# A four-layer kernel on one core: an early one-column GELU, another order on GpSimd, and a copy moved to VectorE

## The reference, cut to what matters

```
f1: windowed attention: q, k, v = x @ w; tau = sigmoid(q.k / sqrt(8)) over the 16 tokens before;
    msg = tau.v; y = x + msg @ wo; layernorm
f2: softmax attention over the batch groups, out projection, layernorm; then 8 experts:
    top 2 of the router's softmax, the larger index wins; gelu(h @ w1[e] + b1[e]) @ w2[e] + b2[e]
    of that expert; layernorm(h + moe)
f3: state-space layer: layernorm, in-projection, causal convolution of 4, silu,
    dt = softplus(..), scan over 256 tokens with 16 states, * silu(z), out projection, residual
f4: h = silu(x @ w1) * (x @ w2); h = gelu(h @ h1); h = gelu(h @ h2); h @ w3   (hidden size 512)
```

## Time and profile before

| what | us |
|---|---|
| median of 3 runs | 908.96 |
| the three runs | 908.96, 910.29, 899.03 |
| profiled execution, its own time | 912.69 |
| its span in the trace | 910.9 |
| PE busy | 782.0 (86%) |
| DVE busy | 655.5 (72%) |
| ACT busy | 586.7 (64%) |
| POOL busy | 441.0 (48%) |
| mean granted clock of TensorE | 0.917 |

### The profile page before, as it was taken

How to read it: one execution, slowest core, us unless ns; L and a number is a source line. 1 busy time by engine, 2 the same in 40 slices (tenths; PEclk the granted TensorE clock), 3 DMA queues, 4 the chain that set the end, 5 groups by cost and what they waited for, 6 DMA issues and landing times.

```text
span 910.9 us, 21586 instructions
## 1 busy us (share of the span) xinstructions
PE 782.0 (86%) x8256; PEld 661.9 (73%) x8256; DVE 655.5 (72%) x1974; ACT 586.7 (64%) x1118; POOL 441.0 (48%) x776
## 2 busy tenths in 40 slices
PE   4978863899999999878768679999999999989996
PEld 4877752789989898867546457777778777767885
DVE  3587763777999999763699958686776867775532
ACT  4586861356767676746787569595867949555641
POOL 2477664233656565455588735436353533434101
PEclk9997985559999999999786889999999999999998
DMA  8400001200000000000000000000000000000000
GB/s 271 146 26 20 21 19 51 56 1 2 3 2 3 2 3 2 2 2 1 1 1 0 1 1 1 1 1 13 1 13 1 2 11 1 13 0 12 13 1 24
DMA packets 22406, 16.95 MB, mean 19 GB/s; under 512 B 2848, under 2 KB 20640, under 8 KB 22048
## 3 DMA queue, kind: packets, MB, share of 16 engines
q1 hardware_dynamic: 21296, 14.95, 5.4%
q10 hardware_dynamic: 1008, 0.63, 0.3%
HBM read 11.38 MB, written 4.19 MB: 17 GB/s over the span
## 4 chain that ended last, share of the span: by engine, by line
PE 56%; DVE 20%; ACT 9%; POOL 8%; issue 6%; DMA 1%; ACTq 0%; POOLq 0%; SPq 0%; DVEq 0%
PE ps L1716 9%; PE ps L1718 8%; PE ps L1717 8%; PE ps L1729 7%; PE ps L1796 6%; PE ps L2161 3%; DVE wall L1375 3%; PE ps L1735 2%; PE ps L1711 2%; PE ps L2020 2%; ACT tau L706 1%; ACT hbd L688 1%; PE ps L1789 1%; PE ps L2074 1%; PE ps L1820 1%
## 5 line engine op out<-in xcount | busy, mean ns | idle before, releaser
L1716 PE MATMUL ps<-h_h,wh_h 128*128 128x512 f32 x256 | 106.2, 415 | 1.4 <-DVE raw L1514 1.2
L1718 PE MATMUL ps<-h_l,wh_h 128*128 128x512 f32 x256 | 101.0, 395 | 0.0
L1717 PE MATMUL ps<-h_h,wh_l 128*128 128x512 f32 x256 | 100.8, 394 | 0.0
L1796 PE MATMUL ps<-w_e,he 128*128 128x128 f32 x512 | 78.2, 286 | 12.7 <-ACT he L738 12.3
L1796 PEld LDWEIGHTS ps<-w_e,he 128*128 128x128 f32 x512 | 67.0, 196 | 17.4 <-ACT he L738 16.9
L1729 PEld LDWEIGHTS ps<-mov,hbd 32*128 32x128 f32 x2048 | 77.7, 230 | 1.3 <-issue 1.3
L1729 PE MATMUL ps<-mov,hbd 32*128 32x32 f32 (+1 forms) x2048 | 76.8, 306 | 1.0 <-issue 1.0
L584 POOL TENSOR_TENSOR term<-term 128x224 f32<-128x224 f32 (+2 forms) x48 | 37.9, 790 | 79.0 <-DVE term L1406 76.5
L738 ACT ACTIVATE he<-ps,pp 128x256 f32<-128x256 f32 x128 | 58.6, 472 | 21.2 <-PE ps L1718 19.7
L1514 DVE SCALAR_TENSOR_TENSOR raw<-ps,pp,gate 128x512 f32<-128x512 f32 x32 | 23.8, 749 | 49.5 <-ACT gate L921 49.3
L1375 DVE TENSOR_TENSOR wall<-dec,wall 128x224 f32<-128x224 f32 (+6 forms) x112 | 48.7, 435 | 14.6 <-ACT dec L876 11.3
(11 more groups left out here) (299 smaller groups left out, 2522.8 us busy)
## 6 DMA issues: line engine op xcount, KB each, us to landing
x<-in_x SPq DMA_DIRECT2D x16, 128.0 KB
w_h<-in_w_h SPq DMA_DIRECT2D x2, 1024.0 KB, 8.0
x<-x SPq DMA_DIRECT2D x16, 128.0 KB, 1.8
xB<-x SPq DMA_DIRECT2D x32, 64.0 KB
out_x<-xB SPq DMA_DIRECT2D x32, 64.0 KB
w_m<-in_w_m SPq DMA_DIRECT2D x3, 256.0 KB, 3.5
stage_negsel<-in_c_negsel SPq DMA_DIRECT2D x1, 512.0 KB, 4.9
xB<-in_w_e SPq DMA_DIRECT2D x1, 512.0 KB, 6.0
```

The lines of the kernel that those rows point to most:

```text
L1716: pe.matmul(dst, a_h, b_h, start=start, stop=True, skip_group_check=True)
L1717: pe.matmul(dst, a_l, b_h, start=False, stop=True, skip_group_check=True)
L1718: return pe.matmul(dst, a_h, b_l, start=False, stop=True, skip_group_check=True)
L1796: last = pe.matmul(ps[:, ACC, P * c:P * c + P], he[e % 2][:, P * c:P * c + P], w_e2[:, e, :], start=False, stop=True, skip_group_check=True)
```

## The change

Three edits that do not touch each other:

1. A new tile `gelu_one` of one column. In each expert step ScalarE takes the GELU of the first column of the constant tile `half` into it, between `le` and the third expert's `gelu(n, l, 2)`, whose waits come after it. Nothing reads the result.
2. GpSimd in the last stage. Where a block enters and n < 16, `input_scale` comes first in the step, ahead of `rstd_and_shift` (before: after it). In odd steps from 5 on, `scales(n + 4)` comes after `skips(n)` and `stored(n - 2)` (before: ahead of both). Step 16 and the even steps' `scales` stay as they were.
3. The query's copy from PSUM to `mov` in the first stage leaves ScalarE and is done by VectorE at the end of `values`, behind the transpose to `vT`, with a wait for `a_qk_ps`; it still counts up `a_qT`.

```diff
--- before.py
+++ after.py
@@ -259,6 +259,7 @@
         hT = chan("hT")
 
 
+        gelu_one = sb("gelu_one", [P, 1])
         negsel = sb("negsel", [P, NE, P], F32R)
         b_e2 = sb("b_e2", [P, D])
         w_router = sb("w_router", [P, NE])
@@ -613,23 +614,26 @@
                 entering, leaving = block_of(n, 4), block_of(n, 7)
                 if n == 0:
                     products(1)
+                if entering is not None and n < NB:
+                    input_scale(entering)
                 if have(-2):
                     c_ln2.rstd_and_shift(pool, chain, eps, half, minus, (n - 2) % 4, n - 1)
                 if n == NB:
-                    input_scale(block_of(n, 4))
+                    input_scale(entering)
                     c_ln2.rstd_and_shift(pool, chain, eps, half, minus, (NB - 1) % 4, NB)
-                elif entering is not None:
-                    input_scale(entering)
                 if leaving is not None:
                     output_scale(leaving)
                 if have(0):
                     sums(n)
-                if have(4):
+                odd = n >= 5 and n % 2 == 1
+                if have(4) and not odd:
                     scales(n + 4)
                 if have(0):
                     skips(n)
                 if have(-2):
                     stored(n - 2)
+                if have(4) and odd:
+                    scales(n + 4)
                 if have(2):
                     products(n + 2)
                 if leaving is not None:
@@ -715,7 +719,6 @@
                     act.wait_ge(S["a_m_ps"], n + 1)
                     act.activation(msgT[l][:, :], bank(l, 0, 0, NT), ACT.Copy).then_inc(S["a_msgT"], 1)
                 if have(1):
-                    act.activation(mov[o][:, :], ps[:, 4 * o, 0:NT], ACT.Copy).then_inc(S["a_qT"], 1)
                     act.wait_ge(S["a_vT"], n + 2)
                     spread = flat3(vbd[o][:, :, :]).rearrange("p (k h c) -> p k h c", h=4, c=HD)
                     for h in range(4):
@@ -773,6 +776,7 @@
                     act.wait_ge(S["b_lg"], n + 2)
                     act.activation(le[o][:, :, :], lg[o][:, :, :], ACT.Exp).then_inc(S["b_le"], 1)
                 if have(0):
+                    act.activation(gelu_one[:, :], half[:, 0:1], ACT.Gelu)
                     gelu(n, l, 2)
                     gelu(n, l, 3)
                 if have(5):
@@ -1087,6 +1091,8 @@
 
                     dve.wait_ge(S["a_vbd"], n - 1)
                 dve.transpose(vT[l][:, :], ps[:, b + 2, 0:NT]).then_inc(S["a_vT"], 1)
+                dve.wait_ge(S["a_qk_ps"], n + 1)
+                dve.tensor_copy(mov[l][:, :], ps[:, b, 0:NT]).then_inc(S["a_qT"], 1)
 
             def blocks(t):
                 return t.rearrange("p (b d) -> p b d", d=D)
```

## The result

The changed kernel takes **897.65 us** (median of 20 runs, 892.91 to 903.51), the kernel before beside it on the same chip 904.15 us (20 runs, 899.03 to 910.29): ratio 0.9923 with a 95% interval of 0.9901 to 0.9945, 6.5 us less. That is a real gain, though under 2%. The profiled execution took 897.95 us (span 896.2, granted clock 0.919), against 912.69 (0.917) before. The profiles are thus 14.7 us apart, more than twice the medians. The reader has to find which part of that is the change.

What follows compares the result with a forecast made beforehand. TensorE, busy nearly throughout, was taken to bound the kernel, so its waits must shrink. Gains of 2.2 and 4.6 less 0.35 make 6.5 us, taken off the three-run median 908.96: 902.5 us, range 892 to 910.

Steps and rivals of the forecast that it cites:

- the place drawn: Expert step, ScalarE: the GELU table load starts right behind the small exponential; the third expert's GELU starts 0.88 us earlier.
- TensorE's 0.76 us wait: Expert steps 1 to 9: TensorE's wait for the GELU output, 0.76 us each, 6.8 us in all, would be gone.
- the 0.8 us at `lg`: Expert step: sign that TensorE's wait for VectorE's `lg`, 0.18 us before, would grow to some 0.8 us.
- the 1.5 us for steps 1 to 9: Expert stage: gain taken as most of VectorE's 1.7 us wait for `xh`; bounds 0 and 6.8 us.
- Step 10: Expert stage: this step would add 0.15 us of gain, VectorE being still full up to `lg`.
- step 11: Expert stage: VectorE's work thins out here, so the whole 0.76 us would count as gain.
- The 0.4 us for contention: Last stage: GpSimd's sums beside VectorE's state updates would lose 0.4 us, half of at most 0.2 in four steps.
- the cover: First stage: VectorE's 0.64 us gap waiting for GpSimd hides the query copy; about 0.3 us of it would remain.
- TensorE keeps its 0.76 us: Rival, expert stage: VectorE's gaps shrink, steps 1 to 11 give 8.4 instead of 2.4 us: 896.5 us; chance 0.17.
- Nothing is left: Rival: state updates slow fully or another wait replaces `c_ya`, and the early load gives nothing: 908 us; chance 0.17.
- The added GELU does not help: Rival, expert stage: a drain, or the load still behind the wait; -4 to 0, 904 to 909 us; chance 0.05.
- The copy is not hidden: Rival, first stage: the query copy lengthens all 16 steps, up to 7.2 us, with more half clock: about 915; chance 0.09.

Runs made afterwards that it cites:

- part 1 alone: The kernel before with only the one-column GELU added: 905.47 us against 904.84, ratio 0.9999 [0.9967, 1.0032].
- the other place: The changed kernel with VectorE's copy of `le` into `lg` moved behind the third write of `lg`: 893.58 us against 905.32, ratio 0.9870.
- part 2 alone: The kernel before with only GpSimd's new order in the last stage: 900.74 us against 904.84, ratio 0.9935 [0.9908, 0.9962].
- part 3 alone: The kernel before with only the query's copy moved to VectorE: 903.72 us against 904.84, ratio 0.9982 [0.9958, 1.0006].
- The stretched maximum: The changed kernel with VectorE's copy of `le` into `lg` replaced in place by a maximum of `le` with itself: 899.35 us against 906.92, ratio 0.9929.

## Why the prediction was right, and where its terms were off

The forecast was 902.5 us, 6.5 us under the median of three runs; the medians of 20 runs each differ by 6.5. The measured 897.65 is 4.85 us lower than forecast because the kernel before, by 20 runs, takes 904.15 us and not the 908.96 of the three. The difference is right partly because two terms erred in opposite directions, and to the tenth by luck: the interval of the ratio is a gain of 5.0 to 9.0 us.

**Part 1, forecast 2.2 gained, about 1.0 by the trace** (part 1 alone: 0.9999 [0.9967, 1.0032]). Right: the load goes to the place drawn, TensorE's 0.76 us wait vanishes and comes back elsewhere, and VectorE decides. It comes back in two places, 0.35 us at `t_h` and 0.33 at `lg`, not as the 0.8 us at `lg` that was forecast. The term that failed is the 1.5 us for steps 1 to 9, "most of VectorE's wait". That wait went and the step shortened by 0.01 us, not by the 0.14 that makes a step of 14.9. The sentence behind it, that the rest of the step is VectorE's "own work and the gaps between dependent short instructions", took the length of every instruction for work; 0.17 us of the copy's 0.33 us was waiting for GpSimd, which the 0.167 us at the other place shows. Step 10 gave 0 for 0.15, step 11 gave 0.65 for 0.76; the rest of the 1.0 us is small differences in steps 0 and 13, which no experiment separates.

**Part 2, forecast 4.6 gained, 5.6 by the trace** (part 2 alone: 0.9935 [0.9908, 0.9962]). The mechanism is right in each step. Two sizes are off. The 0.4 us for contention of GpSimd's sums with the state updates did not come: the updates take 0.86 and 0.66 us, before and after. And the waits understate their own cost: taken away, 5.0 us of wait shortened the pairs by 5.6. That is about 0.2 us more per wait. The first product behind the wait was 0.71 us long and is 0.61 without it, and it now starts 0.16 us before the product ahead has ended (670.40):

```profile
669.38 1.02 PE L2057 MATMUL ps<-bbd,wendT 128*128 128x256 f32 x4
670.24 0.61 PE L1741 MATMUL ps<-w_out,c_ya 128*128 128x128 f32 x4
```

**Part 3, forecast 0.35 lost**: not seen in either direction; the cover was read rightly, 0.33 us of the gap being left where about 0.3 was forecast.

**The rivals.** "TensorE keeps its 0.76 us" is refuted in this kernel: the step is 15.02. Its idea, that VectorE's step can shrink, is true, but through the copy and not through earlier work. "Nothing is left" fell for part 2 and nearly came true for part 1. "The added GELU does not help" by a drain is refuted, the load starting 0.02 us behind the exponential. The Trainium skill ("ScalarE: Activation LUTs", What ACT_TABLE_LOAD costs) gives 1283 ns for the load, which these rows confirm, and a drain of about 1380 ns, which they do not show. (With that drain the GELU would, as an estimate, have come at 268.8 and not at 268.33, a loss of about 0.5 us a step and not the 0.35 of the forecast.) "The copy is not hidden" is refuted by part 3 alone.

The Trainium skill ("GPSIMD Engine Reference", Key points) says that VectorE and GpSimd share their way into SBUF. I weighed that where it did not matter, at `hd`, and not at the copy, where it set the step of a whole stage. By the Trainium skill this concerns VectorE instructions in a 2-port mode or with two inputs in SBUF. The stretched maximum (0.613 us) has two such inputs and fits; the copy has one, and no row shows its mode.

## What to carry to other kernels

An engine "full of its own work" may be waiting inside an instruction: compare the mean length of one form and size at several places, and look at what another engine ends at the same moment. Two limits of nearly the same length hide each other, so an edit that removes one measures as nothing; test it again with the other gone before dropping it. On a queue that waits anyway, put the work that is ready ahead of the wait, and count the saving only up to about the wait that it feeds (here 5.6 us for waits of 5.0).

## What the runs showed of the hardware

- A VectorE copy of 128x16 elements from SBUF to SBUF took 0.167 us where GpSimd was idle and 0.611 us beside GpSimd's additions of 128x256. It ended 0.03 us after the addition that ran when it started, whether that was the fourth (0.33 and 0.61 us) or the second (0.56 us). A maximum of the same size took 0.613 us there, MAX8 0.137 us.
- An ACT_TABLE_LOAD of 1.28 us started 0.02 us behind the activation ahead of it, and one column's GELU took 0.20 us, as much as 16 columns of the exponential.
- TensorE's granted clock fell to 1.2 GHz for 3.4 us behind a wait of 1.4 us in the kernel before and stayed at 2.4 GHz in the changed one, with the same wait and the same products behind it. The place in the first stages where the clock fell moved as well; the two together make some 8 of the 14.7 us between the two profiles.
